# ScalarE reads two table places and issues the row loads of the first pair of the first expert pass

## The chip, the cores and the metric

The kernel runs on one core of one Trainium2 chip. The metric is the device time of the whole kernel in microseconds (us). All engines are told by their own names: TensorE (PE in the profile), VectorE (DVE), ScalarE (ACT), GpSimd (POOL) and SyncE (SP), which computes nothing and issues most of the transfers.

## The reference

There are 64 sequences of 256 tokens of 256 numbers each. The first half is a layer normalisation, an attention without a softmax over a context of 120 tokens, and another layer normalisation. The second half routes every token to two of sixteen experts, and each expert is a 256 x 256 matrix with a bias:

```python
x = x + _L0_xattn_ref(ctx_1024, _layernorm(x), Wq, bq, Wk, bk, Wv, bv, gamma, beta)
x = x + _L0_ffn_ref(_layernorm(x), gate_w, expert_w, expert_b)

def _L0_ffn_ref(tokens, gate_w, expert_w, expert_b):
    weights = softmax(tokens @ gate_w.T)
    top2_w, top2_idx = top_k(weights, 2)
    y = relu(einsum('nh,edh->ned', flat, expert_w) + expert_b)
    sel = take_along_axis(y, top2_idx[:, :, None], axis=1)
    return sum(sel * top2_w[:, :, None], axis=1)
```

## The kernel before, in words

**Two halves.** In the first half (64 steps and three to drain, laid out one after the other by `dense_steps`) every batch goes through attention and the gate. GpSimd scatters its rows into the DRAM tensor `bins[0]`, sorted by each token's first expert (line 638, semaphores `s_row`). The rows of one expert end up in one region that is cut into tiles of 128 rows. How many tiles an expert has is only known when the last batch has been counted.

**The table.** After the last batch VectorE works out, in a chain of some twenty small operations, where each of the 144 tiles begins in `bins[0]` and which expert it belongs to. TensorE transposes the result, and VectorE places it in an SBUF tile, `table` (line 1320, semaphore `s_table`). Row 0 holds the first row of each tile for pass 0, and so each load of a tile needs a number of the table in a register of the engine that issues it. `table_reader` (lines 135 to 151) gives a function that loads V = 24 table places into 24 registers with one instruction (line 147, two for the last trip) and then bounds each one (`nc.snap`, line 148).

**Two expert passes.** Pass k = 0 takes tiles by the tokens' first expert, pass k = 1 by the second. A pass has 6 trips of V = 24 tiles, taken as 12 pairs. For each tile:

- SyncE loads 128 rows into a slot of `row_in` (pass 0: `load_first`, line 482; pass 1: `load_second`, line 490). `s_in[j]` tells that pair j has landed. For the very first tile of a pass there is a semaphore of its own, `s_in0`, so that the pair can be taken one tile at a time.
- TensorE transposes the tile (line 835), ScalarE copies it out of PSUM as its head (lines 1028, 1044, 1046), VectorE subtracts the head to get the rest (lines 1324, 1380), TensorE multiplies heads and rests with the expert's weights (lines 857 to 859, six products a tile), ScalarE weighs the result (line 1032), and VectorE adds it to the row (line 1344 in pass 0, lines 1367 and 1376 in pass 1).
- GpSimd scatters the finished tile with an indirect transfer (line 666): in pass 0 to `bins[1]`, sorted by the second expert, and in pass 1 to the result. `s_put[j]` tells that it has landed.

A slot of `row_in` is loaded again when its scatter has landed. Pass 1 reads `bins[1]`, so SyncE waits for all scatters of pass 0 (line 495) before its first load of pass 1.

**The work around the change.** After its last scores TensorE has three runs of matmuls on an idle tile that give no result (`keep_warm`, line 680): 17 before the transposition of the table (line 829), 18 behind it, and 4 between the first transpositions and the first products. Behind the 18 it reads its own 24 places of table row 1 (the experts' offsets), and then it does `first_pair`: transpose tile 0 when `s_in0` says that it has landed, transpose tile 1 when `s_in[0]` does, 4 idle matmuls, the products of tile 0, transpose pair 1, the products of tile 1; then transpose pair 2, the products of pair 1, and so on. SyncE waits at lines 471 to 473 for the last scatters, the filling of the bins and the table, reads 24 places of row 0, and issues all 24 tiles of the first trip in order. ScalarE issues no transfer anywhere in this kernel; its last operation of the first half is an exponential of the last gaps (line 939), and its next is the head of tile 0 (line 1044).

Of the kernel before, what the change touches and what calls it, by code (L numbers as in the profile page):

```python
# [25 lines left out]
P = 128  # L26
NB, S, D = 64, 256, 256
SC = 120
NH = 16
E = 16  # L30
# [8 lines left out]
FULL = D + ROW  # L39
# [4 lines left out]
ROWS = SPARE + E * P  # L44
# [6 lines left out]
PAIRS = V // 2  # L51
# [49 lines left out]
def dense_steps(step, low, high):  # L101

    for s in range(low, high):
        step(Batch(s))
# [12 lines left out]
def pair_number(k, i, j):  # L117

    return i * PAIRS + (k * TRIPS * PAIRS + j)
# [7 lines left out]
def put_count(k, i, j):  # L127

    return slot_uses(k, i, j, 32) - k * 16 * (TILES - FULL_TILES) * (j % PAIRS == PAIRS - 1)


def first_trip(i):

    return isinstance(i, int) and i == 0
# [18 lines left out]
def build(nc, x, ctx_t, wkv_t, wq_t, gate_t, we_t, we_slabs, bkv, be, bq, gamma, beta, out):  # L153
    bins = [nc.dram_tensor("bins0", [ROWS, ROW], F32, kind="Internal").ap(),
            nc.dram_tensor("bins1", [DUMP + 2 * E * P, FULL], F32, kind="Internal").ap()]
# [3 lines left out]
    with ExitStack() as ctx:  # L159
        def sb(name, shape, dt=F32):  # L160
            return ctx.enter_context(nc.sbuf_tensor(name, shape, dt))
# [4 lines left out]
        def sem(name):  # L166
            return ctx.enter_context(nc.semaphore(name))
# [73 lines left out]
        table = sb("table", [8, P], I32)  # L241
# [5 lines left out]
        row_in = sb("row_in", [P, V, FULL])  # L247
# [54 lines left out]
        s_init = sem("dram_fill_written")  # L302
# [8 lines left out]
        s_row = [sem(f"rows_scattered{n}") for n in range(4)]  # L311
# [41 lines left out]
        s_table = sem("table_placed")  # L353
        s_in = [sem(f"row_pair_loaded{n}") for n in range(PAIRS)]
        s_in0 = sem("first_row_tile_loaded")
# [38 lines left out]
        def _(sp):  # L394
# [80 lines left out]

            def load_first(k, i):
                firsts = first_rows(k, i)
                for j in range(PAIRS):
                    if not first_trip(i):
                        sp.wait_ge(s_put[j], put_count(k, i, j))  # L480
                    for t in range(2):
                        sp.dma_start(row_in[:, 2 * j + t, D:FULL], bins[k][bass.ds(firsts[2 * j + t], P), :]  # L482
                                     ).then_inc(s_in0 if first_trip(i) and j + t == 0 else s_in[j], 16)

            def load_second(k, i):

# [16 lines left out]
                else:  # L503
                    for j in range(PAIRS):
                        sp.wait_ge(s_sum2, pair_number(k, i, j) - PAIRS + 1)
                        load_part(j, 0, FULL, s_in[j])

            expert_bodies(sp, load_first, 0, peel_first=1, peel_last=1)
            expert_bodies(sp, load_second, 1, peel_first=1)
            for j in range(PAIRS):  # L510
# [391 lines left out]
        def _(act):  # L902
# [117 lines left out]

            dense_steps(step, -1, NB + 3)

            def head_rows(k, i, j):
                number = pair_number(k, i, j)
                act.wait_ge(s_prt, number + 1)
                if not (isinstance(number, int) and number < RB):
                    act.wait_ge(s_py, number + 1 - RB)
                act.activation(row_head[:, j % RB], ps_rt[j % RB][:], ACT.Copy).then_inc(s_rhead, 1)
# [10 lines left out]
            def first_pairs(k):  # L1039
                number = pair_number(k, 0, 0)  # L1040
                act.wait_ge(s_prt0, k + 1)
                if k == 1:
                    act.wait_ge(s_py, number + 1 - RB)
                act.activation(row_head[:, 0, 0], first_rt[0][:, 0], ACT.Copy).then_inc(s_rhead0, 1)
                act.wait_ge(s_prt, number + 1)
                act.activation(row_head[:, 0, 1], first_rt[1][:, 1], ACT.Copy).then_inc(s_rhead, 1)
                act.wait_ge(s_py0, k + 1)
                weigh_tile(k, 0, 0, first_y[0]).then_inc(s_y0, 1)
                head_rows(k, 0, 1)
                act.wait_ge(s_py, number + 1)  # L1050
                weigh_tile(k, 0, 1, first_y[1]).then_inc(s_y, 1)
                head_rows(k, 0, 2)
                weigh(k, 0, 1)
                head_rows(k, 0, 3)
# [390 lines left out]
```

## Time and profile before

| | us |
|---|---|
| median of three runs | 857.09 (856.97 to 857.63) |
| the profiled execution, its own time | 854.82 |
| its span, first to last instruction | 853.0 |

| engine | busy us | share of the span |
|---|---|---|
| TensorE, matmuls | 746.2 | 87% |
| VectorE | 668.3 | 78% |
| GpSimd | 592.6 | 69% |
| ScalarE | 591.0 | 69% |

The mean granted clock of TensorE is 0.964 of full speed. The shares are means over stages with different limits: the first half ends at about 454 us, the table takes until 456 us, pass 0 lasts from there to about 651 us, and pass 1 to the end. A time in the trace is counted from the start of the span. "PEldq", "SPq" and the like are sequencers, which read registers and issue transfers while the engine's arithmetic goes on or is idle. A chain row names what held the end of the kernel at that time, followed back from the last instruction.

### The profile page before, as it was taken

What the parts mean: (1) busy time and instruction counts of PE and PEld (TensorE: products, weight loads), DVE (VectorE), ACT (ScalarE), POOL (GpSimd) and SP (SyncE); (2) the same over time, 40 slices, a digit from 0 to 9 for tenths busy, and PEclk for the clock granted to TensorE, in tenths of its full rate; (3) what the DMA queues carried; (4) which work ended last, traced back from release to release, by engine and by line L of the source; (5) the groups of instructions that cost most, each with busy time, mean ns of one, the idle gap of its engine ahead of it and who ended that gap; (6) DMA issues with size and microseconds to landing.
All of it is one profiled execution on the core that took longest, in us unless ns stands there. A gap on an engine that the chain in (4) does not pass through costs nothing. (4 is left out here: it accounts for less than half of the span.)

```text
span 853.0 us, 20821 instructions
## 1 busy us (share of the span) xinstructions
PE 746.2 (87%) x5497; PEld 656.0 (77%) x5502; DVE 668.3 (78%) x2218; ACT 591.0 (69%) x1683; POOL 592.6 (69%) x783
## 2 busy tenths in 40 slices
PE   8999999999999999999998989778793899998800
PEld 5887888888888888888875988768772799997800
DVE  6999999999999999999995987677651566765610
ACT  5988899998999999998972665555441566665500
POOL 5585767777777677666662777777774677777774
PEclk9999999999999999999999999999996999999965
DMA  7699988998998887767514999999976999999421
GB/s 203 150 255 312 250 259 245 271 259 249 249 262 250 248 240 222 223 227 232 170 45 136 330 317 323 314 316 318 308 264 215 347 404 404 405 382 319 147 105 68
DMA packets 142892, 218.42 MB, mean 256 GB/s; under 512 B 39103, under 2 KB 74431, under 8 KB 142807
## 3 DMA queue, kind: packets, MB, share of 16 engines
q1 hardware_dynamic: 112999, 131.21, 47.0%
q0 software_dynamic: 29808, 86.20, 33.1%
q8 instruction: 38, 0.62, 0.3%
q14 instruction: 47, 0.39, 0.1%
HBM read 96.36 MB, written 116.80 MB: 250 GB/s over the span
## 5 line engine op out<-in xcount | busy, mean ns | idle before, releaser
L638 POOL DMA_INDIRECT bins<-rows x128 | 129.7, 1013 | 70.3 <-POOL rows L631 46.5
L666 POOL DMA_INDIRECT out_rows<-y,put_at x143 | 138.5, 969 | 56.3 <-issue 39.6
L666 POOL DMA_INDIRECT bins<-row_in,put_at x143 | 138.7, 970 | 56.0 <-issue 48.1
L745 PE MATMUL ps_q<-h_t,wq 128*128 128x256 f32 x512 | 131.7, 379 | 1.3 <-ACT h_t L973 1.3
L745 PEld LDWEIGHTS ps_q<-h_t,wq 128*128 128x128 f32 x512 | 91.6, 189 | 15.0 <-ACT h_t L973 1.7
L1076 DVE BATCH_NORM_STATS2 st<-y 128x6 f32<-128x512 f32 x128 | 89.6, 701 | 5.8 <-DMA y<-in_x 3.7
L1032 ACT ACTIVATE ps_q<-ps_q,row_in 128x256 f32<-128x256 f32 x144 | 58.5, 444 | 50.7 <-PE ps_q L859 50.7
L857 PE MATMUL ps_q<-we_head,row_head 128*128 x288 | 87.8, 305 | 4.3 <-DVE row_rest L1324 4.3
L538 POOL TENSOR_TENSOR c_rest<-c_sb,c_head 128x240 fp32r<-128x240 f32 x64 | 47.8, 747 | 62.5 <-DVE y L1186 58.9
L615 POOL TENSOR_TENSOR y<-y,beta_sb 128x512 f32<-128x512 f32 x64 | 85.3, 1332 | 0.8 <-DVE y L1186 0.8
L858 PE MATMUL ps_q<-we_head,row_rest 128*128 x288 | 81.7, 284 | 0.0
L859 PE MATMUL ps_q<-we,row_head 128*128 x288 | 81.6, 283 | 0.0
L932 ACT ACTIVATE q_t<-ps_q,bq_sb 128x256 f32<-128x256 f32 x128 | 60.3, 471 | 29.0 <-PE ps_q L745 29.0
L767 PEld LDWEIGHTS ps_mg<-wg_centred,h_t 128*128 128x128 f32 x512 | 61.9, 191 | 21.4 <-issue 20.8
L713 PE MATMUL ps_att<-kvm,q_t 128*128 128x128 f32 x512 | 72.8, 285 | 0.6 <-ACT q_t L932 0.6
L965 ACT ACTIVATE y<-y,nmr,rstd 128x256 f32<-128x256 f32 x128 | 69.2, 589 | 0.4 <-DVE nmr L1082 0.4
L767 PE MATMUL ps_mg<-wg_centred,h_t 128*128 128x16 f32 x512 | 66.3, 261 | 1.1
L713 PEld LDWEIGHTS ps_att<-kvm,q_t 128*128 128x128 f32 x512 | 62.3, 192 | 1.0 <-ACT q_t L932 1.0
L857 PEld LDWEIGHTS ps_q<-we_head,row_head 128*128 128x128 f32 x288 | 55.2, 192 | 5.8 <-issue 5.7
L956 ACT ACTIVATE rows<-y,rows 128x256 f32<-128x256 f32 x128 | 58.1, 501 | 2.1
L919 ACT ACTIVATE lnv<-st,eps 128x2 f32<-128x2 f32 x192 | 54.5, 284 | 6.2 <-DVE st L1076 6.1
L1350 DVE COPY put_at<-row_in 128x2 int32<-128x2 int32 x72 | 14.3, 199 | 55.6 <-DMA out_rows<-y,put_at 26.1
(173 smaller groups left out, 2365.5 us busy)
## 6 DMA issues: line engine op xcount, KB each, us to landing
bins<-zeros SPq DMA_DIRECT2D x48, 768.0 KB
row_in<-bins SPq DMA_DIRECT2D x128, 260.0 KB
row_in<-bins SPq DMA_DIRECT2D x160, 132.0 KB, 2.0
y<-in_x SPq DMA_DIRECT2D x64, 256.0 KB, 3.5
c_sb<-in_ctx_t SPq DMA_DIRECT2D x64, 120.0 KB, 3.5
we<-in_we_t SPq DMA_DIRECT2D x8, 512.0 KB, 5.4
we<-be_dram POOLq DMA_DIRECT2D x8, 512.0 KB, 7.9
we<-row_in POOLq DMA_DIRECT2D x8, 512.0 KB, 6.1
```

Source lines behind the costliest of these rows:

```text
L615: pool.tensor_tensor(x_beta[:, n], x_sb[:, s.buf(4)], beta_sb[:].unsqueeze(1).to_broadcast([P, NT, D]), ALU.add).then_inc(s_xb, 1)
L638: pool.indirect_dma_start(out=bins[0], in_=r[:, t, :], out_offset=bass.IndirectOffsetOnAxis(ap=r[:, t, POS_COL:POS_COL + 1].bitcast(I32), ...
L666: pool.indirect_dma_start(out=bins[1] if k == 0 else out, in_=row_in[:, t, :] if k == 0 else y[:, t, :], out_offset=bass.IndirectOffsetOnA ...
L713: mm = pe.matmul(ps_att[:, t, c * P:(c + 1) * P], q_t[:, c, t, :], kvm[:, c, :], start=True, stop=True)
L745: mm = pe.matmul(ps_q[dc][:, 0:S], wq[:, c, dc * P:(dc + 1) * P], h_t[:, c, :, :], start=(c == 0), stop=(c == KC - 1))
L767: mm = pe.matmul(logits[:, t, :], h2_t[:, c, t, :], wg_centred[:, c, :], start=(c == 0), stop=(c == KC - 1))
L857: pe.matmul(o, heads, w_head, start=(c == 0), stop=False)
L858: pe.matmul(o, rests, w_head, start=False, stop=False)
L859: mm = pe.matmul(o, heads, we_rest[:, c, bass.ds(at[2 * j + t], D)], start=False, stop=(c == KC - 1))
L932: act.activation(q_t[:, dc, :, :].rearrange("p t n -> p (t n)"), ps_q[dc][:, 0:S], ACT.Identity, bias=bq_sb[:, dc:dc + 1]).then_inc(s_q, 1)
L965: a = act.activation(h[:, b.buf(4), t, :], x_sb[:, b.buf(4), t, :], ACT.Identity, bias=nmr[:, t:t + 1], scale=rstd[:, 0, b.buf(2), t:t + 1])
L1076: dve.bn_stats(st[:, n, b.buf(2)].rearrange("p t m -> p (t m)"), src.rearrange("p t d -> p d t")).then_inc(s_mv[n], 1)
```

## The change

ScalarE, behind its last step of the first half, waits for the same semaphores as SyncE, reads two places of table row 0 into two registers of its own, and issues the loads of tiles 0 and 1 (pair 0) of pass 0. They signal `s_in0` and `s_in[0]`, as before. SyncE still reads its 24 places, but its first issue is that of tile 2. Pass 1 and all other trips of pass 0 are as they were.

```diff
             def load_first(k, i):
                 firsts = first_rows(k, i)
-                for j in range(PAIRS):
+                for j in range(1 if first_trip(i) else 0, PAIRS):
                     if not first_trip(i):
                         sp.wait_ge(s_put[j], put_count(k, i, j))
                     for t in range(2):
                         sp.dma_start(row_in[:, 2 * j + t, D:FULL], bins[k][bass.ds(firsts[2 * j + t], P), :]
-                                     ).then_inc(s_in0 if first_trip(i) and j + t == 0 else s_in[j], 16)
+                                     ).then_inc(s_in[j], 16)
...
             dense_steps(step, -1, NB + 3)
+
+            for n in range(4):
+                act.wait_ge(s_row[n], 32 * (NB // 4))
+            act.wait_ge(s_init, 2 * 16 * (E // 4 + 2))
+            act.wait_ge(s_table, 1)
+            first_regs = [act.alloc_register(f"first_row_{t}") for t in range(2)]
+            act.load(first_regs, table[0:1, 0:2])
+            for t, landed in enumerate((s_in0, s_in[0])):
+                at = nc.snap(first_regs[t], min_val=0, max_val=ROWS - P)
+                act.dma_start(row_in[:, t, D:FULL], bins[0][bass.ds(at, P), :]).then_inc(landed, 16)
```

## Rows read from the trace of the kernel before

**Rows 1.** Busy time by stage: columns PE, PEld, DVE, ACT, POOL, clock, DMA share, GB/s.
```profile
472.70:648.00 175.30, 141.69 (x1107) 131.26 (x1107) 124.27 (x339) 91.33 (x202) 133.53 (x138) 0.97 0.89 306
648.00:665.00 17.00, 10.16 (x60) 8.36 (x60) 5.12 (x11) 5.48 (x12) 3.81 (x5) 0.70 0.74 226
```

**Rows 2.** GpSimd's timeline: start us, us, what, in brackets the idle time before it.
```profile
465.42 0.97 POOL L666 DMA_INDIRECT bins<-row_in,put_at  x1 [10.65 <-issue]
...
472.66 1.02 POOL L666 DMA_INDIRECT bins<-row_in,put_at  x1 [0.54 <-issue]
```

**Rows 3.** The chain that ended last, from the last scatter: start us, us, what.
```profile
453.81 2.44 DMA bins<-rows
456.46 1.63 SPq L147
458.13 0.20 SPq L148
...
458.85 0.38 SPq L482
459.46 0.37 SPq L482
460.03 0.33 SPq L482
```

**Rows 4.** TensorE's timeline from the idle matmuls to the products of pair 1.
```profile
455.67 3.83 PE L680 MATMUL ps_q<-idle,ones_bf 128*128 128x512 bf16 x17
460.90 0.44 PE L835 MATMUL ps_ht<-ident,row_in 128*128 128x128 f32 x2 [1.40 <-DMA row_in<-bins]
461.61 0.44 PE L835 MATMUL ps_mg<-ident,row_in 128*128 128x128 f32 x2 [0.27 <-DMA row_in<-bins]
461.88 1.03 PE L680 MATMUL ps_q<-idle,ones_bf 128*128 128x512 bf16 x4
462.55 0.47 PE L857 MATMUL ps_att<-we_head,row_head 128*128 x1
...
463.45 0.62 PE L835 MATMUL ps_h2t<-ident,row_in 128*128 128x128 f32 x4
...
464.62 0.60 PE L835 MATMUL ps_mg<-ident,row_in 128*128 128x128 f32 x4
465.58 0.38 PE L857 MATMUL ps_q<-we_head,row_head 128*128 x1 [0.36 <-DVE row_rest L1324]
```

**Rows 5.** Register loads of line 147: ns min/median/max; 24 places each at 456 us.
```profile
L147 PEldq TENSOR_LOAD <-table x1: 1815/1815/1815, 456.3 to 456.3; - x1
L147 SPq TENSOR_LOAD <-table x1: 1629/1629/1629, 456.5 to 456.5; - x1
```

**Rows 6.** The same of the last trip: 8 places (min), then 16 (max).
```profile
L147 SPq TENSOR_LOAD <-table x2: 1137/1320/1504, 593.6 to 594.8; - x2
L147 PEldq TENSOR_LOAD <-table x2: 881/1312/1742, 603.3 to 604.2; - x2
```

**Rows 7.** ScalarE's timeline around its free time.
```profile
450.30 0.23 ACT L939 ACTIVATE exps<-gaps 128x36 f32<-128x36 f32 x1 [2.20 <-DVE gaps L1099]
461.37 0.38 ACT L1044 ACTIVATE row_head<-ps_ht 128x256 fp32r<-128x256 f32 x1 [10.85 <-PE ps_ht L835]
```

**Rows 8.** SyncE's issues of line 482 from 456 to 473 us: ns min/median/max.
```profile
L482 SPq DMA_DIRECT2D row_in<-bins x24: 332/333/1209, 458.9 to 472.4; - x24
```

**Rows 9.** The chain over the boundary to pass 1.
```profile
648.52 2.77 DMA bins<-row_in,put_at
...
651.37 0.34 SPq L490
```

**Rows 10.** TensorE's and GpSimd's timeline in pass 1.
```profile
665.03 0.66 PE L835 MATMUL ps_h2t<-ident,row_in 128*128 128x128 f32 x4 [0.89 <-DMA row_in<-bins]
...
669.87 0.97 POOL L666 DMA_INDIRECT out_rows<-y,put_at  x1 [0.78 <-issue]
...
843.35 0.97 POOL L666 DMA_INDIRECT out_rows<-y,put_at  x1 [0.30 <-issue]
```

## The prediction

> **What bounds the kernel now.** I read the busy time by stage first, then GpSimd's timeline, then the chain of waits around the table. The first view shows that no engine is full in pass 0 except by its own rhythm: between 472.70 and 648.00 us GpSimd has 138 operations, nothing but scatters [rows 1], and its timeline shows them 1.27 us apart, 0.97 busy and 0.30 between two [rows 2, 9]. From the fifth scatter at 472.66 [rows 2] to the last of 143 at 648.52 [rows 9] that is 138 steps, and 175.86 / 138 = 1.274 us each. So GpSimd is never let down in pass 0 once it has begun: pass 0 ends 175.9 us after its fifth scatter begins, whatever the other engines do in between. Whatever brings the fifth scatter forward brings the end of pass 0 forward by the same amount, and nothing else in the pass does.
>
> Next, what leads to that scatter. The last scatter of the first half lands at 456.25 (453.81 + 2.44), and from there SyncE is the chain: it reads 24 places (1.63 us), bounds them and makes the first address (458.13 to 458.85), and issues tile 0, tile 1 and tile 2 at 458.85, 459.46 and 460.03 [rows 3]. TensorE waits for tile 0 until 460.90 and for tile 1 until 461.61 [rows 4]. The reader is to see two things in TensorE's rows. Its idle matmuls end at 459.50 (455.67 + 3.83), so it stands idle for 1.40 us before tile 0. And the first products at 462.55 follow without idle time on the four idle matmuls behind tile 1's transposition, so that it is tile 1's landing, not tile 0's, from which everything behind it hangs: products of tile 0 are 0.94 us behind the transposition of tile 1, pair 1 at 463.45, pair 2 at 464.62, products of pair 1 at 465.58 [rows 4], the first scatter at 465.42 and the fifth at 472.66 [rows 2].
>
> ScalarE, which gets the new work, is idle from 450.53 to 461.37, 10.85 us of them waiting for the transposition of tile 0 [rows 7].
>
> **The change part by part.**
>
> *The wait.* ScalarE waits for the same things as SyncE. Nothing is queued behind it but the head of tile 0, which needs the loads anyway. I put the start of its read at SyncE's, 456.46 [rows 3]. Cost nothing, covered by ScalarE's idle 10.85 us.
>
> *The read of two places.* The trace has no read of two places; it has 24, 16 and 8. At 456 us, 24 cost SyncE 1.63 and TensorE 1.82 us [rows 5]. In the last trip 8 and then 16 places cost SyncE 1.14 and 1.50 us, TensorE 0.88 and 1.74 [rows 6]. That gives 0.046 us a place for SyncE ((1.504 - 1.137) / 8) and 0.108 for TensorE ((1.742 - 0.881) / 8). From SyncE's 24 places in the same stretch, 22 fewer leave 1.63 - 22 x 0.046 = 0.62. From TensorE's 8, six fewer leave 0.88 - 6 x 0.108 = 0.23. The upper end is SyncE's 8 places as they stand, 1.14. I take 0.65, near the first, since it starts from the stretch in question.
>
> *The bounds and the addresses.* SyncE spends 458.85 - 456.46 - 1.63 = 0.76 us between read and first issue, on bounding 24 registers and one move [rows 3]. Its first row of line 148 is 0.20 us. ScalarE bounds one register before each of its two issues. I take 0.15 for each bound and 0.15 for move and gaps (ends: 0 and 0.20 a bound).
>
> *The two issues.* Tile 0 then goes out at 456.46 + 0.65 + 0.15 + 0.15 = 457.41. SyncE's second issue is 0.61 behind its first [rows 3]; with one bound in between, tile 1 goes out at 457.41 + 0.61 + 0.15 = 458.17. For SyncE, tile 1 took 461.61 - 459.46 = 2.15 us from issue to TensorE's start, tile 0 took 2.05 [rows 3, 4]. ScalarE's tile 1 is therefore transposed at 458.17 + 2.15 = 460.32 instead of 461.61: **1.29 us earlier**. Tile 0 would be ready at 459.46, just where the idle matmuls end, and costs nothing. With a read of 0.23 and bounds of nothing, tile 1 comes at 459.60 (2.0 earlier); with 1.14 and 0.20, at 460.91 (0.7 earlier). On ScalarE the issues end at about 458.5, before its next operation at 461.37 - 1.29 = 460.08; a cover of 1.5 us.
>
> *SyncE.* Its read is as long as before, and tile 2 takes the place of tile 0 at 458.85, tile 3 that of tile 1, and so on: every later tile of the first trip is two issues, 1.18 us, earlier (460.03 - 458.85). Pair 1 is ready at 461.61, and is wanted at 463.45 - 1.29 = 462.16. Pair 2 is ready some 1.2 to 1.4 us later, at about 463.0, and is wanted at 463.33, and behind it the products of pair 1 have 0.36 us of slack that VectorE makes [rows 4]. So the supply holds, but it is next in line: it caps the gain at 463.45 - 461.61 = 1.84 us by pair 1 and about as much by pair 2. SyncE has one issue of 1.21 us among the 24 [rows 8]; it is a later one, and when GpSimd has its rhythm it has cover.
>
> *TensorE's own read* (1.82 us from 456.3 [rows 5]) ends at 458.1, and with the same 0.7 us of bounding at 458.8, still under the idle matmuls that end at 459.50. Three engines now read the table at once where there were two. If this cost each 0.2 us, TensorE would not notice, and pair 1 would still be in time (461.81 against 462.16).
>
> *From there to the end.* Products, heads, rests and sums follow on each other at fixed distances, so the fifth scatter starts at 472.66 - 1.29 = 471.37. GpSimd itself had 0.24 us to spare there (0.54 idle instead of 0.30 [rows 2]), all of which moves with the rest. Pass 0 ends 1.29 us earlier. The boundary is a chain of a landing (2.77 us) and of SyncE's issues from 651.37 on [rows 9], which moves as it is. In pass 1 TensorE waits for SyncE's supply again (0.89 us at 665.03) before GpSimd's last real start at 669.87, and then scatters until 843.35 [rows 10]. All of it hangs from SyncE's first issue at 651.37, so the gain passes through whole: one pair of loads is moved once, and it is worth 1.29 us once.
>
> **A page that speaks against it.** What the trace has: SyncE's issues take 0.33 to 0.38 us each, and a tile is 2.05 us on its way [rows 3, 4]. The Trainium skill, page "DMA: Bandwidth & Descriptors", section "Issuing engines are not separate DMA queues", says that issuing from several engines at once saves only the time that the sequencer needs to start the transfer. By that rule, the change would be worth at most the two issues, and nothing for tiles 0 and 1, which were SyncE's first already. The rows bear it out for the transfer, but what is cut here lies ahead of the issue. The same page, section "Latency and other measured facts", puts the floor of a register load at about 600 ns; with it the gain would be 1.34 us. No read in this trace is that short.
>
> **The rivals.**
>
> *A. The read is no shorter.* If reading two places cost nearly what 24 do, only the bounding of 22 registers is saved: 0.76 - 0.30 = 0.46 us, less 0.15 for the second bound, a gain of 0.3, and 856.8 us. For it: SyncE's 8 places cost 1.14, most of its price is fixed. Against: TensorE's 8 cost half of its 16 [rows 6], and a read of 1.14 already leaves 0.7.
>
> *B. ScalarE's first transfer is slow, and the kernel is slower.* ScalarE issues none before, so its first one is priced by no row. It decides at a delay of 1.29 us over SyncE's behaviour; beyond that tile 1 comes later than now, and GpSimd with it. The nearest rows are SyncE's longest issue, 1.21 instead of 0.38 [rows 8], and a scatter's way of 2.77 instead of 2.05 us [rows 9]: together 1.55 us, tile 1 0.26 us later than now, 857.4 us. To be slower by over 0.2%, 3.0 us of delay are needed. For it: nothing but that it is the first. Against: it is the same kind of transfer with the same shapes.
>
> *C. More than that.* With a short read (0.23) and short bounds the gain is 2.0, capped at 1.84 by SyncE's supply. Besides, the granted clock in 648 to 665 us is 0.70 on the mean [rows 1]: TensorE, idle at the boundary, runs its first products of pass 1 at 1.2 GHz. Were the rise to fall more favourably, some of this comes back, though TensorE's 0.89 us of waiting at 665.03 [rows 10] hides most of it. Gain 1.75 to 2.1, 855.2 us.
>
> **How the numbers follow.** The profiled execution took 854.82, its span 853.0; 1.29 less gives a profiled 853.5. It lies 2.27 below the median of the runs, and the same 1.29 less than the median is 857.09 - 1.29 = **855.8 us**. About 0.2% (1.7 us) is what a measurement of this kernel can tell from no change, and the forecast lies inside it. Chances: forecast (gain 0.7 to 1.7) 0.66; A 0.10; B 0.09, of which 0.05 beyond 0.2% slower; C 0.15. To C's 0.15 comes 0.02 of the forecast's upper edge: faster 0.17, slower 0.05, same 0.78. The range goes from 855.0 (2.1 gained, which is C with its clock) to 857.2 (A, and B up to the slow issue alone).
>
> **What would show each step.** In the profile after: a register read on ScalarE at 456.5 of 0.5 to 0.9 us; ScalarE's two issues at about 457.4 and 458.2; SyncE's first issue at 458.85 as before, of tile 2; tile 0 transposed at 459.5, tile 1 at 460.3; pair 1 and pair 2 without a wait for their landing; the first scatter at 464.1, the fifth at 471.4, the last of pass 0 at 647.2, and no other gap in between. It is wrong if ScalarE's issue takes over 1 us, if TensorE waits at pair 1 or 2, or if GpSimd's rhythm of 1.27 us is broken anywhere, since then pass 0 is not bound as I say.

## The result, and the profile after

The changed kernel took 854.38 us in the median of thirteen runs (852.18 to 856.01), against 856.96 for the kernel before in thirteen runs of the same session (854.77 to 858.50). The ratio is 0.9978, with a 95% interval of 0.9968 to 0.9987: some 1.9 us less, and by the interval 1.1 to 2.7. The ratio is not the quotient of the two medians, which is 0.9970 (2.58 us less); in the runs below, too, the two figures differ, by up to 0.0014, and the text goes by the ratio and its interval. The forecast was 1.29 us less. Its range of 855.0 to 857.2 stood on a median of 857.09 before; that median times the ratio is 855.2 us, inside the range, while the median of 854.38 as it stands lies below it. The profiled execution took 853.38 us with a span of 851.6, 1.4 less than before.

Single executions of one and the same program differ by some 4 us here, more than the whole effect. What the change does is therefore read from distances within a trace, and the ratio is used only to see that it agrees.

The chain of the changed kernel, from the last scatter of the first half to the transposition of tile 1 (start us, us, what). It answers to [rows 3]:

```profile
453.80 2.43 DMA bins<-rows
...
456.47 0.68 ACTq L1028
457.15 0.03 issue
457.18 0.04 ACTq L1030
...
457.31 0.39 ACTq L1031
...
457.87 2.22 DMA row_in<-bins
460.09 0.04 issue
460.13 0.33 PE ps_mg L835
```

SyncE has gone from the chain. ScalarE reads its two places in 0.68 us, issues tile 0 at 457.31 and tile 1 at 457.87. TensorE's timeline, which answers to [rows 4], and SyncE's first issues, now of tile 2 and on:

```profile
459.55 0.38 PE L835 MATMUL ps_ht<-ident,row_in 128*128 128x128 f32 x2
460.13 0.44 PE L835 MATMUL ps_mg<-ident,row_in 128*128 128x128 f32 x2 [0.20 <-DMA row_in<-bins]
460.40 1.03 PE L680 MATMUL ps_q<-idle,ones_bf 128*128 128x512 bf16 x4
461.08 0.47 PE L857 MATMUL ps_att<-we_head,row_head 128*128 x1
...
461.98 0.60 PE L835 MATMUL ps_h2t<-ident,row_in 128*128 128x128 f32 x4
...
463.24 0.66 PE L835 MATMUL ps_mg<-ident,row_in 128*128 128x128 f32 x4
```

```profile
458.75 1.51 SPq L482 DMA_DIRECT2D row_in<-bins  x3
```

TensorE's 1.40 us of idle time before tile 0 is gone (its idle matmuls end at 459.72), and tile 1 is transposed 1.48 us earlier. GpSimd's timeline, which answers to [rows 2, 9, 10]:

```profile
463.95 0.96 POOL L666 DMA_INDIRECT bins<-row_in,put_at  x1 [9.18 <-issue]
...
471.16 1.02 POOL L666 DMA_INDIRECT bins<-row_in,put_at  x1 [0.54 <-issue]
...
647.18 0.97 POOL L666 DMA_INDIRECT bins<-row_in,put_at  x1 [0.30 <-issue]
...
668.60 0.97 POOL L666 DMA_INDIRECT out_rows<-y,put_at  x1 [0.94 <-issue]
```

The fifth scatter is 1.50 us earlier, the last of pass 0 1.34 earlier. The page of the profile has a new queue, `q10 hardware_dynamic: 288, 0.27, 0.1%` in its list: ScalarE's two transfers.

The first half ends at another time in every execution (the last scatter lands between 455.8 and 459.4 us in the traces of this study), so from here on times are counted from the end of SyncE's wait for that landing, called W. One row for each trace, us:

| kernel | W | tile 1 transposed | fifth scatter | last of pass 0 | fifth to last |
|---|---|---|---|---|---|
| before | 456.26 | 5.34 | 16.40 | 192.26 | 175.86 |
| before, again | 456.90 | 5.39 | 16.61 | 192.46 | 175.85 |
| changed | 456.25 | 3.87 | 14.90 | 190.93 | 176.02 |
| changed, again | 456.96 | 3.71 | 14.76 | 190.62 | 175.87 |
| SyncE alone | 456.71 | 3.90 | 16.64 | 192.60 | 175.95 |
| ScalarE reads 24 | 459.36 | 5.39 | 16.42 | 192.38 | 175.96 |
| ScalarE later | 456.39 | 7.96 | 20.12 | 195.97 | 175.85 |
| both issue | 456.72 | 3.83 | 15.00 | 190.75 | 175.76 |
| two idle matmuls | 456.53 | 3.76 | 15.24 | 191.20 | 175.95 |

### The profile page after: what moved, and what is told of

Its sections match the earlier page's. It is cut to its first block and busy times, and to the rows that moved or that the text cites. A ratio compares the mean times of both kernels' runs of the same rounds, so it can differ in the third digit from the quotient of the medians.

```text
span 851.6 us, 20831 instructions
## 1 busy us (share of the span) xinstructions
PE 750.2 (88%) x5501; PEld 659.5 (77%) x5502; DVE 668.6 (79%) x2218; ACT 590.9 (69%) x1683; POOL 593.5 (70%) x783
```

## The experiments

**The two kernels again.** 

> The kernel before, unchanged, as if it were a change: how far the comparison itself wanders, and a second trace of it. Counted from the end of SyncE's wait for the last scatter of the first half (456.26 us in the first trace of before): fifth scatter of pass 0 16.4 us later, last scatter 192.3 later. Ratio within 0.9985 and 1.0015 of 1. If the boundary (last scatter of pass 0 to first of pass 1) is 11.2 us again, where the traces of the changed program have 10.5 to 11.0, a part of the measured gain comes from there; if it is 10.5 to 11.0 too, it does not.

Measured: ratio 1.000 (0.9991 to 1.001). The second trace of before agrees with the first up to the end of pass 0 within 0.2 us (table).

> The changed kernel as it is, for its time beside the others of this study. My theory (the gain is how much earlier tile 1 of pass 0 lands, 1.48 us in the first trace, and it is carried 1:1 to the end by GpSimd's rhythm): fifth scatter of pass 0 at 471.2 us, last at 647.2, 1.4 us less than before, ratio 0.9984. Rival (the first comparison's 2.6 us are real and half of them come from elsewhere, for example from the clock at the boundary): ratio 0.997 or less, and a boundary from the last scatter of pass 0 to the first of pass 1 that is shorter than the 11.2 us of before by a microsecond.

Measured: 855.20 us, ratio 0.9979 (0.9963 to 0.9994); fifth scatter at W + 14.76, last of pass 0 at W + 190.62. A run meant as a delay turned out to be a third copy of the changed program, since its extra reads are not in it (below); it has 0.9979 (0.9961 to 0.9997), and W + 14.78 and W + 190.72. The mean of the three traces of the changed program is 190.76, that of the two of before 192.36: **1.60 us, or 0.19%**, are gained by the end of pass 0. The intervals of all three comparisons contain that. So the measured 0.21 to 0.22% needs no second source. Each interval by itself contains 0.997 as well, the value from which the rival above (a second source of gain) began, so the ratios alone do not rule it out; what speaks against it is that all three come out at 0.9978 or 0.9979, and that the boundary is not a microsecond shorter: from the last scatter of pass 0 to the first of pass 1 it is 11.2 and 10.6 us before, 10.95, 10.5 and 10.96 after.

Where executions differ behind that point, one thing is seen. From the last scatter of pass 0 to the last of pass 1 the five traces of the two programs take 194.7 to 194.8 us or 196.6. Both at 196.6 (before again, changed again) have this stretch in pass 1; columns are PE, PEld, DVE, ACT, POOL, granted clock, DMA share, GB/s. First the changed kernel's second trace, then its first:

```profile
672.80:676.20 3.40, 3.40 (x17) 3.40 (x18) 0.69 (x1) 0.60 (x1) 2.49 (x4) 0.50 1.02 390
```

```profile
672.80:676.20 3.40, 3.31 (x29) 3.11 (x29) 2.05 (x4) 1.76 (x5) 2.53 (x3) 1.00 1.04 399
```

TensorE runs at 1.2 GHz for 3.4 us, and GpSimd then stands before its thirteenth scatter of pass 1 until 31.1 us behind the last of pass 0, where the others have 29.1 to 29.3. From the thirteenth to the last, all five need 165.5 to 165.7 us, so the 1.9 us between the traces arise before it. In the third copy the clock fell too, some 0.8 us earlier, and it took 194.8, so the fall alone does not decide it; a second difference is a wait of 1.04 and 1.06 us for the landing of pair 4 that only the two slower traces have. Both kernels have traces with the stop and without. Whether the change makes it rarer, five traces cannot tell. Two of the traces below lie between: SyncE alone (thirteenth at 30.2, last at 196.2) and two idle matmuls (30.1 and 195.8).

**The reads that were not there.** The edit, and what was expected:

```diff
+            spare_regs = [act.alloc_register(f"spare_{t}") for t in range(V)]
+            for _ in range(3):
+                act.load(spare_regs, table[0:1, 0:V])
             first_regs = [act.alloc_register(f"first_row_{t}") for t in range(2)]
```

> As the changed kernel, but ScalarE makes three more reads of 24 places, whose registers nobody uses, before its read of two: tile 1 is some 5.0 us later (3 x 1.65), at 465.1 us. My theory (pass 0 has no slack behind its start): fifth scatter at 476.1 to 476.2, last of pass 0 at 652.2, 3.6 us more than before, 860.6 us, ratio 1.0042. Rival (slack in the 175 us of pass 0 or at the boundary takes some of it up, so that the slope is under 1): under 2.5 us more than before although the fifth scatter is 3.5 us late.

Measured: 854.83 us, the changed kernel's time. The trace has a single read on ScalarE, that of two places:

```profile
L1031 ACTq TENSOR_LOAD <-table x1: 689/689/689, 458.0 to 458.0; - x1
```

Reads into registers that nobody uses are not in the program that ran. The run says nothing about slack; it was made again in another way.

**ScalarE later, with work that stays.** 

```diff
+        s_delay = sem("delay_step")
...
+            for n in range(5):
+                act.activation(h_t[:], h_t[:], ACT.Copy).then_inc(s_delay, 1)
+                act.wait_ge(s_delay, n + 1)
             first_regs = [act.alloc_register(f"first_row_{t}") for t in range(2)]
```

> As the changed kernel, with five operations of ScalarE on an idle tile (128x512), each waiting for the one before, between its waits and its read: the first pair goes out some 3.5 us later than in the changed kernel. My theory (no slack behind the start of pass 0): tile 1 is transposed 7.4 us behind the end of SyncE's wait (changed kernel 3.9, before 5.35), the fifth scatter 18.4 behind it (14.9, 16.4), the last 194.3, and the kernel takes 2.0 us more than before, ratio 1.0024. Rival (slack in pass 0 or at the boundary): the last scatter under 193.3, ratio under 1.001.

Measured: ratio 1.004 (1.0025 to 1.0055), 859.67 us. The last scatter of pass 0 is at W + 195.97, 3.6 us behind before, and 3.6 / 857 is 0.42%. So the start of pass 0 has no slack: what its fifth scatter is late (20.12 - 16.5 = 3.6), the kernel is longer. The fifth-to-last column of the table says the same in nine traces: 175.8 to 176.0 us, whatever happened before.

What missed is the size. Tile 1 is 2.6 us later than before, but the fifth scatter 3.6. TensorE's timeline and granted clock, columns as above:

```profile
463.70 0.69 PE L836 MATMUL ps_ht<-ident,row_in 128*128 128x128 f32 x2 [4.06 <-DMA row_in<-bins]
464.35 0.69 PE L836 MATMUL ps_mg<-ident,row_in 128*128 128x128 f32 x2
464.83 1.91 PE L681 MATMUL ps_q<-idle,ones_bf 128*128 128x512 bf16 x4
466.19 0.71 PE L858 MATMUL ps_att<-we_head,row_head 128*128 x1
```

```profile
459.80:463.30 3.50, 0.00 (x0) 0.00 (x0) 0.00 (x0) 0.08 (x1) 0.00 (x0) 1.00 0.76 223
463.30:466.70 3.40, 3.00 (x9) 1.64 (x10) 1.49 (x6) 0.77 (x2) 0.00 (x0) 0.50 0.99 308
```

TensorE was idle for 4.06 us, was granted 1.2 GHz from 463.3 to 466.7, and the first products came 1.8 us behind tile 1's transposition instead of 0.94. In before it was idle for 1.40 us and stayed at 2.4 GHz (granted clock 1.00 from 459.50 to 467.00). Here the delay cost more than its length, once the clock fell.

**Is it the short read?** ScalarE reads 24 places instead of two.

```diff
-            first_regs = [act.alloc_register(f"first_row_{t}") for t in range(2)]
-            act.load(first_regs, table[0:1, 0:2])
+            first_regs = [act.alloc_register(f"first_row_{t}") for t in range(V)]
+            act.load(first_regs, table[0:1, 0:V])
```

> As the changed kernel, but ScalarE reads 24 places in place of two before it issues the first pair. My theory (the shorter read is the larger part of the gain, line 147's 1.63 us against 0.68): tile 0 goes out at about 458.3 us and tile 1 at 458.9, tile 1 is transposed at 461.1, the fifth scatter starts at 472.1 to 472.2, gain 0.5 us. Rival (what counts is that two engines issue, not what they read; the rule that several issuing engines save issue time alone): if later tiles being two issues earlier were the gain, the fifth scatter would start at 471.2 to 471.5 here too.

Measured: 856.27 us, ratio 0.9992 (0.9977 to 1.0007); fifth scatter at W + 16.42, as before the change. The whole gain is gone, not only the 1.0 us by which the read is longer (1.68 against 0.68). The chain shows where the other 0.5 us went:

```profile
459.58 1.68 ACTq L1028
...
461.42 0.39 ACTq L1031
...
461.98 2.74 DMA row_in<-bins
464.71 0.04 issue
464.76 0.33 PE ps_mg L835
```

Tile 1 goes out at 461.98, W + 2.62, which is 0.58 us earlier than in before, but it is 2.74 us on its way instead of the changed kernel's 2.22. SyncE's tile 2 went out at 461.87 (the trace's first issue of line 482) and was in front of it. So my theory was right that the read is what matters, and the rival, that two issuing engines as such bring the gain, falls: two engines issued here too, and tile 2 went out at W + 2.51, as early as in the changed kernel. The size that I expected, 0.5 us of gain left, was wrong, because I had let ScalarE's and SyncE's transfers pass each other freely.

**Is ScalarE needed?** SyncE makes the short read itself, issues pair 0, and then reads all 24.

```diff
             sp.wait_ge(s_table, 1)
+            first_regs = [sp.alloc_register(f"first_row_{t}") for t in range(2)]
+            sp.load(first_regs, table[0:1, 0:2])
+            for t, landed in enumerate((s_in0, s_in[0])):
+                at = nc.snap(first_regs[t], min_val=0, max_val=ROWS - P)
+                sp.dma_start(row_in[:, t, D:FULL], bins[0][bass.ds(at, P), :]).then_inc(landed, 16)
             first_rows = table_reader(nc, sp, table, 0, ROWS - P)
...
-            for n in range(4):
-                act.wait_ge(s_row[n], 32 * (NB // 4))
-            act.wait_ge(s_init, 2 * 16 * (E // 4 + 2))
-            act.wait_ge(s_table, 1)
-            first_regs = [act.alloc_register(f"first_row_{t}") for t in range(2)]
-            act.load(first_regs, table[0:1, 0:2])
-            for t, landed in enumerate((s_in0, s_in[0])):
-                at = nc.snap(first_regs[t], min_val=0, max_val=ROWS - P)
-                act.dma_start(row_in[:, t, D:FULL], bins[0][bass.ds(at, P), :]).then_inc(landed, 16)
```

> ScalarE issues nothing; SyncE itself reads two places first, issues tiles 0 and 1, then reads all 24 places and goes on with tile 2. My theory (short read gives the first pair early, but SyncE's supply is next in line): tiles 0 and 1 are transposed as early as with ScalarE (459.5 and 460.1 us), but tile 2 goes out at about 460.5 instead of 458.75, so TensorE waits at pair 1 until about 463.3 and at pair 2 and pair 4, and the fifth scatter starts at 472.3 to 473.2, against 472.66 before: nothing gained, at most 0.3 us, or up to 0.6 lost. Rival (only the first pair's landing counts): fifth scatter at 471.2, gain 1.4 us.

Measured: 857.59 us, ratio 1.0012 (0.9995 to 1.0029), fifth scatter at W + 16.64. SyncE's chain, then GpSimd's timeline:

```profile
456.91 0.68 SPq L475
...
458.78 1.42 SPq L147
...
461.18 0.34 SPq L487
```

```profile
464.43 0.97 POOL L671 DMA_INDIRECT bins<-row_in,put_at  x1 [9.20 <-issue]
467.14 0.96 POOL L671 DMA_INDIRECT bins<-row_in,put_at  x1 [1.75 <-DVE row_in L1349]
470.33 1.01 POOL L671 DMA_INDIRECT bins<-row_in,put_at  x1 [2.23 <-DVE row_in L1349]
```

Tile 1 is as early as with ScalarE (W + 3.90), and the first scatter with it. But tile 2 goes out at W + 4.47, 2.0 us later than in the changed kernel (W + 2.50), TensorE waits 1.30 us for pair 1, and by the fifth scatter everything is lost. This shows the second half of the theory: the short read is worth something only because the long one goes on beside it on another engine.

**Both engines at once.** ScalarE reads four places and issues tiles 0, 2 and 3; SyncE reads one and issues tile 1.

```diff
-                for j in range(1 if first_trip(i) else 0, PAIRS):
+                for j in range(2 if first_trip(i) else 0, PAIRS):
...
+            second_reg = sp.alloc_register("second_row")
+            sp.load([second_reg], table[0:1, 1:2])
+            at_one = nc.snap(second_reg, min_val=0, max_val=ROWS - P)
+            sp.dma_start(row_in[:, 1, D:FULL], bins[0][bass.ds(at_one, P), :]).then_inc(s_in[0], 16)
...
-            act.load(first_regs, table[0:1, 0:2])
-            for t, landed in enumerate((s_in0, s_in[0])):
+            act.load(first_regs, table[0:1, 0:4])
+            for t, landed in ((0, s_in0), (2, s_in[1]), (3, s_in[1])):
```

> ScalarE reads four places and issues tiles 0, 2 and 3; SyncE reads one place, issues tile 1 at the same time as ScalarE issues tile 0, then reads 24 and goes on with tile 4. Theory 1 (transfers of two engines share a line, 0.55 to 0.7 us a tile, as in the run in which ScalarE's tile 1 was overtaken by SyncE's tile 2): tile 1 lands 3.6 to 3.85 us behind the end of SyncE's wait although it is issued at 1.1 instead of 1.6; fifth scatter 14.7 to 14.9, no gain over the changed kernel. Theory 2 (the queues are independent at this load): tile 1 lands at 3.2 to 3.4, is transposed straight behind tile 0 at 3.5, fifth scatter at 14.4.

Measured: 855.06 us, ratio 0.9983 (0.9974 to 0.9992), fifth scatter at W + 15.00. The chain:

```profile
457.60 2.63 DMA row_in<-bins
460.23 0.04 issue
460.27 0.44 PE ps_ht L839 x2
460.71 0.22 PE ps_mg L839 x2
```

Both tiles go out at W + 0.88. Tile 0 needs 2.63 us to land instead of the changed kernel's 2.1, and tile 1 is transposed straight behind it, at W + 3.83, no earlier than in the changed kernel, although it was issued 0.7 us sooner. So the transfers share a line (theory 1), and it is tile 0 that pays: it is transposed at W + 3.55 instead of 3.30, the rest of tile 0 is ready at 461.58, and the first products follow at 461.73, W + 5.01 instead of 4.7 to 4.8. The fifth scatter is 0.1 to 0.2 us later than in the changed kernel.

**What the idle matmuls hide.** The last number is `WARM_ROWS`.

```diff
-WARM_START, WARM_ATTEND, WARM_H2, WARM_GATE, WARM_TABLE, WARM_LOADS, WARM_BOUNDARY, WARM_ROWS = 12, 7, 4, 6, 17, 18, 36, 4
+WARM_START, WARM_ATTEND, WARM_H2, WARM_GATE, WARM_TABLE, WARM_LOADS, WARM_BOUNDARY, WARM_ROWS = 12, 7, 4, 6, 17, 18, 36, 2
```

> As the changed kernel, with 2 instead of 4 idle matmuls between the first transpositions and the first products (in both passes). My theory (tile 1's landing counts because four idle matmuls, 0.86 us, stand behind its transposition; the rest of tile 0 would be ready 0.2 to 0.3 us before they end): in pass 0 the first products follow tile 1's transposition by 0.65 to 0.75 us instead of 0.95, the fifth scatter comes 14.5 to 14.7 us behind SyncE's wait instead of 14.75 to 14.95. In pass 1 the idle matmuls run at half the clock (1.91 us for four): first scatter of pass 1 up to 0.9 us earlier, and the seventh unchanged, as it waits for pair 5. Rival (what counts is tile 0's or tile 1's head and rest, not the idle matmuls): no difference in pass 0.

Measured in one execution only, of 854.98 us (the median of before beside it is 856.19). TensorE's timeline, then VectorE's:

```profile
460.29 0.44 PE L835 MATMUL ps_mg<-ident,row_in 128*128 128x128 f32 x2
460.57 0.59 PE L680 MATMUL ps_q<-idle,ones_bf 128*128 128x512 bf16 x2
461.22 0.38 PE L857 MATMUL ps_att<-we_head,row_head 128*128 x1
```

```profile
460.65 0.42 DVE L1390 TENSOR_TENSOR row_rest<-ps_ht,row_head 128x256 fp32r<-128x256 f32 x1 [4.17 <-ACT row_head L1054]
```

A miss. The products follow tile 1 by 0.93 us, with two idle matmuls as with four: the rest of tile 0 ends at 461.07, and they start 0.15 us behind it. The second trace of the changed kernel, with four idle matmuls, has the same 0.15 us (rest at 461.53, products at 461.68), so there, too, tile 0 was the limit; in its first trace the distance is 0.27. And the fifth scatter is later, at W + 15.24, because TensorE then waited 0.38 us for pair 3: SyncE's supply, the next in line. That this wait comes from the fewer idle matmuls is not shown: TensorE was ready for pair 3 at W + 9.49, while the traces of the changed kernel took it up at W + 9.3 to 9.4, and there is one trace. In pass 1 the first scatter is 10.1 us behind the last of pass 0 instead of 10.5 to 11.0, and the seventh at 21.4 is unchanged, as expected.

**The same idea at the second boundary.** Loads of pass 1 on ScalarE, on top of the change. First all four of pair 0, which SyncE then leaves out:

```diff
+                if k == 1:
+                    for j in range(PAIRS):
+                        act.wait_ge(s_put[j], put_count(1, 0, j))
+                    for low, high, landed in ((D, FULL, (s_in0, s_in[0])), (0, D, (s_part[0], s_part[0]))):
+                        for t in range(2):
+                            act.dma_start(row_in[:, t, low:high], bins[1][t * P:(t + 1) * P, low:high]
+                                          ).then_inc(landed[t], 16)
```

> As the changed kernel, and in pass 1 ScalarE, idle there too, issues the four loads of pair 0 (tile 0, tile 1, and their partial sums), so that SyncE starts with pair 1. My theory (the boundary hangs from SyncE's issues at 0.474 us each, and GpSimd's last real start there, its seventh scatter of pass 1, waits for pair 5's landing): pair 1 to 5 land up to 1.9 us earlier, TensorE's wait of 0.8 us before pair 5 goes, and the seventh scatter of pass 1 comes 20.5 to 20.8 us behind the last of pass 0, in place of 21.4. Rival (the transfers, not the issues, are full: 0.74 of the DMA engines busy over the boundary): 21.2 or more, nothing gained.

> The kernel in which ScalarE also issues the four loads of pair 0 of pass 1, once more, to see whether its ratio of 0.9966 with five runs stands against 0.9978 and 0.9979 of the changed kernel. Theory 1 (what its trace shows: TensorE's wait at pair 5 is gone, but tile 0 of pass 1 lands 0.7 us later as it shares the line with SyncE's pair 1, and the two cancel): the last scatter of pass 1 comes 194.7 to 196.6 us behind the last of pass 0, as in all others, ratio 0.9975 to 0.9985. Theory 2 (it spares the second stop that some executions make at the thirteenth scatter of pass 1, 29.5 instead of 31.1 us behind the last of pass 0, and so gains on the mean): 13th scatter at 29.5 again, ratio under 0.9975.

Measured: 854.13 us (0.9966, 0.9952 to 0.9979) with five runs and 853.75 us (0.9974, 0.9963 to 0.9985) with nine. TensorE's wait before pair 5 is gone in both traces, but tile 0 of pass 1, issued together with SyncE's tile 2, is transposed 5.9 us behind the last scatter of pass 0 instead of 5.0, and the first scatter comes at 12.0 and 12.1 us instead of 10.5 to 11.0. The seventh is at 21.9 and the last at 195.3 and 195.2, between the 194.7 and 196.6 of the others. GpSimd has no stop at all behind its third scatter, thirteenth at 29.5 both times, which speaks for theory 2; but 0.9974 is under its bound of 0.9975 by only 0.0001, and the interval holds theory 1's values and the changed kernel's 0.9978. Whether this kernel beats the changed one stays open.

Then the partial sums of pairs 0 and 1, behind ScalarE's heads of pair 0 (SyncE leaves these four out), and the same with two idle matmuls:

```diff
                 act.activation(row_head[:, 0, 1], first_rt[1][:, 1], ACT.Copy).then_inc(s_rhead, 1)
+                if k == 1:
+                    for j in range(PAIRS):
+                        act.wait_ge(s_put[j], put_count(1, 0, j))
+                    for t in range(4):
+                        act.dma_start(row_in[:, t, 0:D], bins[1][t * P:(t + 1) * P, 0:D]
+                                      ).then_inc(s_part[t // 2], 16)
```

> As the changed kernel, and in pass 1 ScalarE issues the partial sums' loads of pairs 0 and 1 (4 transfers), behind its heads of pair 0, so that SyncE has 4 issues fewer ahead of pair 5 and nothing is put in front of tiles 0 and 1. Theory (issues limit the boundary, and the loss in the run with pair 0 on ScalarE was only that SyncE's pair 1 shared the line with tile 0): tile 0 of pass 1 is transposed 5.0 us behind the last scatter of pass 0, as before, TensorE's wait at pair 5 goes, the seventh scatter of pass 1 comes 20.0 to 20.8 us behind the last of pass 0 instead of 21.4 to 21.8, and the kernel takes 0.6 to 1.4 us less than the changed one: ratio 0.9965 to 0.9973. Rival (the transfers are full): seventh scatter at 21.2 or later, ratio 0.998.

> The two before this together. Theory: they add up where the seventh scatter of pass 1 no longer waits for a landing: seventh scatter 19.6 to 20.6 us behind the last of pass 0, fifth scatter of pass 0 at 14.6 behind SyncE's wait, ratio 0.9955 to 0.997. Rival (fewer idle matmuls let the clock rise later at the boundary): the first products of pass 1 stay at 1.2 GHz a stretch longer and the seventh scatter is no earlier than with the parts' loads alone.

Measured: 855.16 us (0.9983, 0.9966 to 0.9999) and 855.51 us (0.9978, 0.9962 to 0.9994): no gain over the changed kernel, against what both theories expected. VectorE's timeline of the first, in pass 1:

```profile
659.23 0.17 DVE L1367 COPY put_at<-row_in 128x2 int32<-128x2 int32 x1 [5.07 <-DMA row_in<-bins]
```

and from its chain:

```profile
653.77 0.35 ACTq L1062
...
654.15 5.05 DMA row_in<-bins
```

The partial sums of pair 0 were issued at 653.8 and 654.15 and landed at 659.2, 5 us later, behind the transfers that SyncE had issued meanwhile, every 0.47 us from 649.93 on (SyncE's own took 2.1 to 5.1 us there). VectorE waited for them with everything behind it, and the seventh scatter came 23.9 us behind the last of pass 0 instead of 21.4. The same in the second (23.8). The last scatter of pass 1 is 197.3 and 197.1 us behind the last of pass 0 in these two traces, 0.5 to 2.6 later than in before and the changed kernel; the ratios, with intervals of 0.16% to either side, show no such loss. The load that was moved to another queue had lost its place in the line, and that was not in my theory.

## Why the prediction was right, and where it was not

*The wait and the read.* ScalarE's read began at W + 0.21 (assumed: 0.20), and took 0.68 us where 0.65 was taken from the slope of SyncE's reads [rows 5, 6]. Rival A (no shorter read) is out, and so is rival C's read of 0.23. The Trainium skill's page "DMA: Bandwidth & Descriptors", section "Latency and other measured facts", puts the floor of a register load at about 600 ns; two places took 0.68 us, but one place on SyncE took 0.47 and four on ScalarE 0.50 in the run in which both issue, so the measurement goes below it.

*The bounds and the issues.* I charged 0.30 us between read and issue and 0.76 between the two issues; they were 0.16 and 0.56. A bound of one register costs 0.04 us, not 0.15. These two terms are 0.34 us less than charged; the read (0.03), its start (0.01) and the transfer (0.11) took 0.15 us more, and so tile 1 came 0.19 us earlier than forecast (460.13, not 460.32).

*The transfer.* 2.26 us from issue to TensorE for tile 1, 2.15 assumed. Rival B (a slow first transfer on ScalarE) is out: tile 0, the first, took 2.1 us from issue to landing, and SyncE's tile 0 took 2.05. Its price was wrong all the same. The delayed run shows that lateness costs more than itself, by the clock, and the runs with both engines that a transfer's way depends on what the other queue has just issued.

*SyncE's supply.* Named as next in line, and so it was: pairs 1 and 2 were in time in the changed kernel, pair 1 too late where SyncE alone did the work, pair 3 in the one trace with fewer idle matmuls.

*"Tile 1's landing, not tile 0's."* Half right. With two idle matmuls the products wait for the rest of tile 0, and in one of the two traces of the changed kernel shown here they do so with four; so tile 0's chain ends within 0.2 us of the idle matmuls. Both landings had to come earlier for the gain, and both did.

*GpSimd's rhythm to the end of pass 0.* Right, and the firmest point: 175.8 to 176.0 us in all traces. Fifth scatter forecast at 471.37, measured 471.16; last at 647.2, measured 647.18.

*The rest.* The gain passed through the boundary as forecast, as far as traces of like kind tell: the last scatter of pass 1 is at W + 387.1 before and W + 385.5 and 385.7 after in the traces without the stop, 389.1 and 387.3 in those with it. One reading in the forecast was wrong: the seventh scatter of pass 1, at 669.87, is not GpSimd's last real start. It stands idle again before the thirteenth, 0.56 us in the first trace of before and 2.10 in the second, so this stop alone varies by more than the gain. 1.29 us were forecast, 1.60 is what five traces give for the end of pass 0. That is inside the forecast's band of 0.7 to 1.7. The ratio's 1.9 us lies in rival C's band (1.75 to 2.1), but its interval of 1.1 to 2.7 covers both. The missing 0.3 are the bounds and the issues (0.19 at tile 1 in the first trace) and some 0.1 us of scatter between traces. Rival C's share at the boundary (a luckier clock) is not shown: the boundary is as long as before.

*The page against it.* The Trainium skill's page "DMA: Bandwidth & Descriptors", section "Issuing engines are not separate DMA queues", says that issuing from several engines saves only the time to start a transfer, and that all of them interleave on the same engines of the DMA. The second half agrees with the runs, in which transfers of the two queues delay each other (2.74 us instead of 2.22, 2.63 instead of 2.1). The first undersells this change: by it the first pair would have gained nothing, and it gained 1.48 us, since SyncE's register read stood in front of its issue. In the run in which ScalarE reads 24 places the rule holds and nothing is gained.

## What to carry to other kernels

When a transfer waits for a number, count the register read and the bounding in front of its issue as well as the issue: an engine that needs two places of a table could issue 1.5 us before the one that reads 24 (457.31 against 458.85), but only if the long read goes on elsewhere. Look for what is bound at a fixed rhythm behind the start, since there a microsecond at the start is a microsecond at the end. And do not move a load to a second queue for its issue time alone: in these runs the transfers of both queues stood in one line, and whatever was issued in front of the first wanted one, or together with it, delayed it by 0.5 us and more.

## What the runs showed of the hardware that I had not expected

- Two queues, one line: ScalarE's tile 1, issued 0.11 us behind SyncE's tile 2, took 2.74 us instead of 2.22; of two tiles issued at the same moment, tile 0 took 2.63 us instead of 2.1; loads issued behind SyncE's stream took 5 us, as did the slowest of SyncE's own.
- At the start of pass 0 a register read of 24 places takes 1.4 to 1.8 us, of two 0.68, of one 0.47, of four 0.50 (on later trips of before, 24 took up to 3.35); reads whose registers are not used are not in the program.
- After 4.06 us of idle time TensorE was granted 1.2 GHz for 3.4 us, and the first products came 0.9 us later than at 2.4 GHz. After 1.40 us of idle time it stayed at 2.4 GHz.
- A stretch of 3.4 us at 1.2 GHz early in pass 1 is there in some executions of both kernels. The two traces that take 196.6 us for pass 1 have it, and one that takes 194.8.
